# Keys of two chunks made together from pieces of the contraction, and the first norm of four tiles on ScalarE, in a post-norm transformer layer on eight cores

## The chip, the cores and the metric

The kernel runs on the 8 NeuronCores of one Trainium2 chip, one program on all of them, each core with its own data. The metric is the device time of the slowest core, in microseconds (us). Cores 0 to 3 are on one die, 4 to 7 on the other; the program has no exchange between cores.

## The reference

The layer takes x of shape (2, 4096, 2048) in fp32. `attn` and `ffn` stand for the two inner functions.

```python
def attn(x):                       # grouped keys and values, 4 groups of 128
    Q = x @ WQ.T + bQ              # 2048 wide, 16 heads of 128
    K = tile(x @ WK.T + bK)        # 512 wide, repeated 4 times
    V = tile(x @ WV.T + bV)        # 512 wide, repeated 4 times
    scores = einsum('btd,bsd->bts', Q, K)      # over all heads at once
    p = softmax(where(causal, -inf, scores)) / sqrt(128)
    return (p @ V) @ proj
def ffn(x):                        # 5632 wide
    h = silu((x @ gate_w.T) * gate_s) * ((x @ up_w.T) * up_s)
    return (h @ down_w.T) * down_s
x = layernorm(x + attn(x))
x = layernorm(x + ffn(x))
```

Since the keys are the same for all four repeats and the scores sum over all heads, the kernel folds WQ over its four repeats (three additions) and does the same with proj, so that queries, keys and values are all 512 wide.

## The kernel before

Four cores share one sequence of 4096 rows. Each core makes keys and values of the whole sequence for itself, in 8 chunks of 512 rows, and owns 8 tiles of 128 query rows, one from each chunk. Chunks 0 to 5 get real keys; chunks 6 and 7 are scored through the query times WK instead.

**Phases.** First keys (`k_outer`, `k_group`) and values (`v_outer`, `v_group`) of chunks 0 to 5, then the queries (`q_batch` for tiles 0 to 3, `q_tile` for the others), then attention of tiles 3, 2, 1, 0 and then 7, 6, 5, 4, each with scores, exponentials, transposes, values, projection, residual and norm; then gate and up of the feed-forward (L756), and last down (L939) with the second norm. The order on every engine is the order in which the program is written; a wait is on a semaphore of the writer.

**The start.** x and the weights lie in HBM in fp32 and are cast to bf16 by the transfers of the GpSimd queue (`load_piece`, L210). `wk` and chunk 0 (`xch[0]`) come in five pieces each, in turn, cut along the contraction at 0, 4, 8, 12, 14 and 16 of its 16 steps (`cuts0`). Chunk 1 is issued once the third piece of `wk` is there, `wv` once the last piece of chunk 0 is there, chunk 2 once the second piece of `wv` is there. `k_outer` makes the keys of a chunk with the pieces in the outer loop and the four column blocks `dq` in the inner one, so each block adds into its own PSUM bank; chunk 0 uses banks 0 to 3 and chunk 1 banks 4 to 7.

**The folds.** The fp32 pieces of WQ and proj (1 MB each, 32 of them) come on the SyncE queue into staging tiles `stg`, and VectorE folds each (L263 and L266) between its other work. `stage` issues the next load into a tile when its fold is done. `folds(n)` puts n of them at that place of VectorE's order.

**The norm.** `norm_a(i)` makes the reciprocal deviation on ScalarE (L701, L702), normalizes `y1` (fp32, 128 x 2048) on VectorE in place (L704) and stores it to `x1fd` (L707). `norm_b(i)` makes the bf16 copy `x1b` on ScalarE (L711), which `turn_x1` transposes on TensorE (L722). `load_xq` (L492) then fetches the residual of a later tile into the same `y1` buffer: tile order[m] goes into `y1` 0 or 1 in turn, and its load waits for the store of tile order[m-2]. SyncE issues stores and residual loads in program order.

Of the kernel before, what the change touches and what calls it, by code (L numbers as in the profile page):

```python
# [14 lines left out]
CT = 16  # L15
# [74 lines left out]
def build_program():  # L90
# [80 lines left out]
    def small(name, shape, dt=F32, size=4):  # L171
        nonlocal o
        t = sb(name, shape, dt, o)
        o += -(-math.prod(shape) * size // 32) * 32 / KB
        return t
# [16 lines left out]
    lnv = small("lnv", [2])  # L192
    rstd = small("rstd", [2])
    st2 = sb("st2", [NT, 5, 6], F32, 204)
    mv2 = sb("mv2", [NT, 2], F32, 205)
# [25 lines left out]
    for p, (lo, hi) in enumerate(zip(cuts0, cuts0[1:])):  # L221
        load_piece(wk, wkd, lo, hi, "wk%d" % p, t_wk)
        load_piece(xch[0], xT[0], lo, hi, "xa%d" % p, t_x[0])
    load_x(1, [t_wk[8]])
    for p in range(4):
        load_piece(wv, wvd, 4 * p, 4 * p + 4, "wv%d" % p, t_wv, [t_x[0][15]])
    load_x(2, [t_wv[7]])
# [43 lines left out]
    def folds(n):  # L271
        for _ in range(n):
            fold()
# [47 lines left out]

    def k_outer(j, cuts, b0):

        for lo, hi in zip(cuts, cuts[1:]):
            for dq in range(4):
                for ct in range(lo, hi):
                    tm = mm_k(j, dq, ct, b0 + dq, [t_wk[ct], t_x[j][ct]], ct == CT - 1)
                if hi == CT:
                    evac_k(j, dq, b0 + dq, tm)

# [46 lines left out]

    k_outer(0, cuts0, 0)
    k_outer(1, [0, 4, 8, 12, 16], 4)
    v_outer(0, 0)  # L380
# [5 lines left out]
    for j in range(1, HI):  # L386
# [24 lines left out]
        if j == 5:  # L411
            load_x(6, [t_kv[4], t_own[4], t_wq[12]])
            load_wkn(0, tk)
            load_x(7, [t_kv[5], t_own[5]])
            q_batch()
            q_tile(5, 5)
            folds(3)

# [280 lines left out]
    def norm_a(i):  # L699
        b, h = buf1[place[i]], place[i] % 2  # L700
        t1 = P.se(lambda e: e.activation(out=lnv[:, h:h + 1], in_=ve_[:, h:h + 1], func=AF.Ln), [t_stat[i]])  # L701
        t1 = P.se(lambda e: e.activation(out=rstd[:, h:h + 1], in_=lnv[:, h:h + 1], func=AF.Exp,  # L702
                                         scale=-0.5), [t1])
        t_n[i] = P.ve(lambda e: e.tensor_scalar(  # L704
            out=y1[b][:], in0=y1[b][:], scalar1=mv[:, h, 0:1], scalar2=rstd[:, h:h + 1],
# [3 lines left out]
    def norm_b(i):  # L709
        m, b = place[i], buf1[place[i]]  # L710
        t_x1b[i] = P.se(lambda e: e.activation(out=x1b[:], in_=y1[b][:], func=AF.Copy),  # L711
                        [t_n[i], t_xb_free, t_z[NT - 1]])
        if m + 2 < 6:
            load_xq(m + 2)
# [64 lines left out]
    v_group(6, 0, 0)  # L779
    folds(1)  # L780
    scores(3)
# [316 lines left out]
```

How the kernel before makes its waits and increments, by code:

```python
                def body(e, items=items):  # L74
                    seen = {}
                    for fn, waits, name, k in items:
                        for s, v in waits:
                            if seen.get(s, 0) < v:
                                e.wait_ge(self.sems[s], v)
                                seen[s] = v
                        if fn is not None:
                            ins = fn(e)
                            if name is not None:
                                ins.then_inc(self.sems[name], k)
```

## Time and profile before

| | us |
|---|---|
| three runs, median (lowest, highest) | 1292.86 (1292.38, 1535.46) |
| the profiled execution | 1292.36 |
| its span on core 7, the slowest | 1290.8 |
| spans of the eight cores | 1286.8 to 1290.8 |
| TensorE busy on core 7 | 1256.3 (97%) |
| VectorE busy | 328.7 (25%) |
| ScalarE busy | 172.9 (13%) |
| TensorE waiting for transfers at the start | 20.0 |

The span runs from the first to the last instruction of the core; the profiled execution's time is 1.6 us more than it. The highest of the three runs stands far above the two others, which agree within 0.04%. TensorE is busy for 97% of the span, so the profile is read for the places where it is not, and for what ends its waits there.

### The profile page before, as it was taken

Reading aid. Unit: us, or ns where it says so; the run is one execution under the profiler, and the core shown is the slowest. Engines: PE = TensorE matmul, PEld = TensorE weight load, DVE = VectorE, ACT = ScalarE, POOL = GpSimd, SP = SyncE. Lnnn points to the kernel's source line nnn. Section 1 sums busy time; section 2 is a strip of 40 time slices with the busy share of each in tenths; the row PEclk is TensorE's granted clock in tenths of the full one; section 3 lists DMA queues with packets and bytes.
Section 4 is the critical chain, followed back from the end, with each engine's and each line's share of the span. In section 5 each row is a group of like instructions: output and inputs, shape, how many; then the busy total and the mean of one; then the engine's idle time right before and its main releaser. Section 6 shows DMA issues by size and latency. Waiting matters only on the chain.

```text
span 1290.8 us, 15305 instructions; the slowest of 8 cores (1286.8 to 1290.8 us)
## 1 busy us (share of the span) xinstructions
PE 1256.3 (97%) x6316; PEld 589.7 (46%) x6316; DVE 328.7 (25%) x537; ACT 172.9 (13%) x269; POOL 73.9 (6%) x140
## 2 busy tenths in 40 slices
PE   4999999999999999999999999999999999999997
PEld 1444445654544444444444444444444444444444
DVE  0044435656873111011011011011010040130435
ACT  0100002333553101101101101100100000000001
POOL 2110000000000000001000000000000000000000
PEclk9999999999999999999999999999999999999999
DMA  9999999866881745545955445445405446464544
GB/s 145 166 254 267 235 195 268 247 152 117 222 221 73 131 67 88 87 86 91 169 103 88 72 69 90 71 69 88 71 1 115 79 70 145 79 143 80 120 124 189
DMA packets 33748, 166.10 MB, mean 129 GB/s; under 512 B 3984, under 2 KB 4112, under 8 KB 20240
## 3 DMA queue, kind: packets, MB, share of 16 engines
q0 software_dynamic: 19584, 96.48, 45.4%
q1 hardware_dynamic: 13808, 67.30, 15.4%
q10 hardware_dynamic: 288, 1.34, 0.3%
q8 instruction: 51, 0.84, 0.2%
q14 instruction: 17, 0.14, 0.0%
HBM read 244.80 MB, written 16.78 MB: 203 GB/s over the span
## 4 chain that ended last, share of the span: by engine, by line
PE 95%; DMA 3%; DVE 1%; issue 1%; ACT 0%; POOL 0%; DVEq 0%; ACTq 0%; POOLq 0%
PE pb L756 47%; PE pb L939 24%; PE pb L302 7%; PE pb L297 5%; PE pb L622 2%; PE pb L676 2%; PE pb L504 2%; DMA wk<-wkd 1%; DMA xch<-xT 1%; PE pb L366 1%; PE pb L351 1%; PE pb L510 1%; PE pb L563 1%; PE pb L454 1%; PE pb L722 0%
## 5 line engine op out<-in xcount | busy, mean ns | idle before, releaser
L756 PE MATMUL pb<-x1T,gu 128*128 128x512 bf16 x2816 | 609.1, 379 | 0.0
L756 PEld LDWEIGHTS pb<-x1T,gu 128*128 128x128 bf16 x2816 | 275.4, 98 | 331.0
L939 PE MATMUL pb<-dT,hT 128*128 128x512 bf16 (+2 forms) x1436 | 304.3, 375 | 0.4 <-DVE hT L774 0.4
L939 PEld LDWEIGHTS pb<-dT,hT 128*128 128x128 bf16 x1436 | 140.0, 98 | 164.8 <-issue 0.9
L774 DVE SCALAR_TENSOR_TENSOR hT<-pb,usc,sil 128x512 bf16<-128x512 f32 x88 | 66.1, 751 | 515.8 <-PE pb L756 515.8
L768 ACT ACTIVATE sil<-pb,gsc 128x512 f32<-128x512 f32 x88 | 60.5, 687 | 513.0 <-PE pb L756 512.9
L297 PE MATMUL pb<-xch,wk 128*128 128x512 bf16 x384 | 87.7, 389 | 20.0 <-DMA xch<-xT 20.0
L302 PE MATMUL pb<-wv,xch 128*128 128x512 bf16 x448 | 98.2, 379 | 0.0
L967 DVE SCALAR_TENSOR_TENSOR y<-pb,dsb 128x512 f32<-128x512 f32 x32 | 22.1, 691 | 216.0 <-PE pb L939 215.7
L297 PEld LDWEIGHTS pb<-xch,wk 128*128 128x128 bf16 x384 | 38.1, 100 | 68.5 <-issue 26.3
L302 PEld LDWEIGHTS pb<-wv,xch 128*128 128x128 bf16 x448 | 43.7, 98 | 52.4
L749 POOL DMA_DIRECT2D gu<-gud x46 | 26.0, 566 | 629.3 <-PE pb L756 587.5
L293 DVE TENSOR_TENSOR vv<-pb,bvb 128x512 bf16<-128x512 f32 x28 | 19.3, 690 | 120.2 <-PE pb L302 120.1
L263 DVE TENSOR_TENSOR stg<-stg 128x1024 f32<-128x1024 f32 x32 | 39.1, 1222 | 37.5 <-DMA stg<-wqd 25.9
L905 POOL DMA_DIRECT2D dT<-dnd x44 | 23.2, 534 | 286.3 <-PE pb L939 285.9
L985 ACT ACT_TABLE_LOAD x1 | 1.3, 1283 | 268.0 <-DVE lv L982 268.0
L504 PE MATMUL pb<-kT,qT 128*128 128x512 bf16 x132 | 32.2, 378 | 3.0 <-DVE lsc L517 1.7
L622 PE MATMUL pb<-vv,pt 128*128 128x512 bf16 x140 | 34.0, 379 | 1.0 <-DVE pt L569 1.0
L287 ACT ACTIVATE kT<-pb,bkc 128x512 bf16<-128x512 f32 x24 | 16.2, 687 | 124.0 <-PE pb L297 124.0
L676 PE MATMUL pb<-pjs,zT 128*128 128x512 bf16 x128 | 30.2, 379 | 0.0
L210 POOL DMA_DIRECT2D xch<-xT x33 | 17.7, 554 | 150.6 <-PE pb L297 54.6
L680 DVE SCALAR_TENSOR_TENSOR y<-pb,rec,y 128x512 f32<-128x512 f32 x32 | 23.1, 746 | 4.0 <-PE pb L676 1.3
(98 smaller groups left out, 453.2 us busy)
## 6 DMA issues: line engine op xcount, KB each, us to landing
gu<-gud POOLq DMA_DIRECT2D x46, 1024.0 KB, 10.3
dT<-dnd POOLq DMA_DIRECT2D x44, 512.0 KB, 6.3
stg<-wqd SPq DMA_DIRECT2D x16, 1024.0 KB, 24.6
stg<-prd SPq DMA_DIRECT2D x16, 1024.0 KB, 10.7
xch<-xT POOLq DMA_DIRECT2D x31, 512.0 KB, 17.6
y<-xq SPq DMA_DIRECT2D x8, 1024.0 KB, 8.3
x1fd<-y SPq DMA_DIRECT2D x8, 1024.0 KB, 7.2
x1r<-x1fd SPq DMA_DIRECT2D x4, 2048.0 KB, 14.2
```

Of the source, the lines that this page charges most:

```text
L263: t1 = P.ve(lambda e: e.tensor_add(stg[b][:, 0:2, :], stg[b][:, 0:2, :], stg[b][:, 2:4, :]), [tl])
L297: return P.pe(lambda e: e.matmul(bank[bk][:], wk[:, ct, dq * 128:(dq + 1) * 128], xch[XB[j]][:, ct, :], start=(ct == 0), stop=(ct == CT - ...
L302: return P.pe(lambda e: e.matmul(bank[bk][:], xch[XB[j]][:, ct, sv * 128:(sv + 1) * 128], wv[:, ct, :], start=(ct == 0), stop=(ct == CT - ...
L504: tm = P.pe(lambda e, c=c, dq=dq, bk=bk: e.matmul(bank[bk][:], qT[:, dq, i * 128:(i + 1) * 128], kT[c][:, dq, :], start=(dq == 0), stop=(d ...
L622: tm = P.pe(lambda e, c=c, r=r, j=j, first=first, last=last: e.matmul(bank[Z_BANK][:], pt[r][:, j, :], vv[c][:, j, :], start=first, stop=l ...
L676: tm = P.pe(lambda e, d=d: e.matmul(bank[pb][:], zT[i % 4][:, d, :], pjs[:, d, c * 512:(c + 1) * 512], start=(d == 0), stop=(d == 3)), [bf ...
L749: gu_at[it] = (s, P.dma("gpsimd", lambda e: e.dma_start(out=gu[s][:], in_=gud[it]), "gu%d" % s, list(waits) + [t_gu_free[s]]))
L756: tm = P.pe(lambda e, ct=ct: e.matmul(bank[bk][:], gu[s][:, w, ct, :], x1T[tch][:, ct, :], start=(ct == 0), stop=(ct == CT - 1)), [tg, bf[ ...
L768: ta = bf[gb] = P.se(lambda e: e.activation(out=sil[s][:], in_=bank[gb][:], func=AF.Silu, scale=gsc[:, it:it + 1]), [tm, t_sil[s], t_c["gs ...
L774: t_h[it][tch] = bf[ub] = t_sil[s] = P.ve(lambda e: e.scalar_tensor_tensor(out=hT[tch][:, it, :], in0=bank[ub][:], scalar=usc[:, it:it + 1 ...
L905: t_dT[s] = P.dma("gpsimd", lambda e: e.dma_start(out=dT[s % 8][:], in_=dnd[s // 11, s % 11]), "dT%d" % (s % 8), waits)
L939: return P.pe(lambda e: e.matmul(bank[tt if bk is None else bk][:, 0:hi - lo], hT[tt // 4][:, it, (tt % 4) * 128:(tt % 4 + 1) * 128], dT[s ...
```

## The change

1. `cuts0` also cuts chunk 1: its pieces are issued right behind those of `wk` and chunk 0, without a wait. `k_outer` works on both chunks for each piece of the contraction: 16 matmuls of chunk 0 (banks 0 to 3), 16 of chunk 1 (banks 4 to 7), and so on.
2. `wv` is issued when the fourth piece of chunk 0 (steps 12 and 13) is there, no longer the fifth.
3. One fold moves on VectorE from behind the first value group of chunk 6 (ahead of `scores(3)`) into the batch of queries: `folds(3)` becomes `folds(4)`.
4. For tiles 3 to 0 `norm_a` ends with a 128 x 1 instruction on VectorE (`nb`, minus mean times reciprocal deviation). `norm_b` makes `x1b` from the raw `y1` on ScalarE with scale and bias, then `y1` itself in place in a second pass, and only then issues the store. Tiles 7 to 4 are as before.

```diff
     for p, (lo, hi) in enumerate(zip(cuts0, cuts0[1:])):
         load_piece(wk, wkd, lo, hi, "wk%d" % p, t_wk)
         load_piece(xch[0], xT[0], lo, hi, "xa%d" % p, t_x[0])
-    load_x(1, [t_wk[8]])
+        load_piece(xch[1], xT[1], lo, hi, "xb%d" % p, t_x[1])
     for p in range(4):
-        load_piece(wv, wvd, 4 * p, 4 * p + 4, "wv%d" % p, t_wv, [t_x[0][15]])
+        load_piece(wv, wvd, 4 * p, 4 * p + 4, "wv%d" % p, t_wv, [t_x[0][13]])
...
-    def k_outer(j, cuts, b0):
+    def k_outer(cuts):
         for lo, hi in zip(cuts, cuts[1:]):
-            for dq in range(4):
-                for ct in range(lo, hi):
-                    tm = mm_k(j, dq, ct, b0 + dq, [t_wk[ct], t_x[j][ct]], ct == CT - 1)
-                if hi == CT:
-                    evac_k(j, dq, b0 + dq, tm)
+            for j in range(2):
+                for dq in range(4):
+                    for ct in range(lo, hi):
+                        tm = mm_k(j, dq, ct, 4 * j + dq, [t_wk[ct], t_x[j][ct]], ct == CT - 1)
+                    if hi == CT:
+                        evac_k(j, dq, 4 * j + dq, tm)
...
-    k_outer(0, cuts0, 0)
-    k_outer(1, [0, 4, 8, 12, 16], 4)
+    k_outer(cuts0)
...
             q_tile(5, 5)
-            folds(3)
+            folds(4)
...
+        if i < 4:
+            t_n[i] = P.ve(lambda e: e.tensor_scalar(
+                out=nb[:, h:h + 1], in0=mv[:, h, 0:1], scalar1=rstd[:, h:h + 1], scalar2=-1.0,
+                op0=OP.mult, op1=OP.mult), [t1])
+            return
...
     def norm_b(i):
-        m, b = place[i], buf1[place[i]]
-        t_x1b[i] = P.se(lambda e: e.activation(out=x1b[:], in_=y1[b][:], func=AF.Copy),
-                        [t_n[i], t_xb_free, t_z[NT - 1]])
+        m, b, h = place[i], buf1[place[i]], place[i] % 2
+        if i < 4:
+            t_x1b[i] = P.se(lambda e: e.activation(
+                out=x1b[:], in_=y1[b][:], func=AF.Identity, scale=rstd[:, h:h + 1], bias=nb[:, h:h + 1]),
+                [t_n[i], t_xb_free, t_z[NT - 1]])
+            t_n[i] = P.se(lambda e: e.activation(
+                out=y1[b][:], in_=y1[b][:], func=AF.Identity, scale=rstd[:, h:h + 1], bias=nb[:, h:h + 1]),
+                [t_x1b[i]])
+            t_st1[i] = P.dma("sync", lambda e: e.dma_start(out=x1f_r[i], in_=y1[b][:]), "x1f%d" % b,
+                             [t_n[i]])
+        else:
+            t_x1b[i] = P.se(lambda e: e.activation(out=x1b[:], in_=y1[b][:], func=AF.Copy),
+                            [t_n[i], t_xb_free, t_z[NT - 1]])
...
     v_group(6, 0, 0)
-    folds(1)
     scores(3)
```

The start on TensorE, before (`xch_66`, `xch_67` and `xch_68` are the buffers of chunks 0, 1 and 2; L297 makes keys, L302 values):

```order
L297 MATMUL pb<-xch_66,wk 128x512 x64
L297 MATMUL pb<-xch_67,wk 128x512 x64
L302 MATMUL pb<-wv,xch_66 128x512 x64
L302 MATMUL pb<-wv,xch_67 128x512 x64
L297 MATMUL pb<-xch_68,wk 128x512 x64
```

The same place of the changed kernel, whose line numbers are one higher here:

```order
L298 MATMUL pb<-xch_66,wk 128x512 x16
L298 MATMUL pb<-xch_67,wk 128x512 x16
L298 MATMUL pb<-xch_66,wk 128x512 x16
L298 MATMUL pb<-xch_67,wk 128x512 x16
L298 MATMUL pb<-xch_66,wk 128x512 x16
L298 MATMUL pb<-xch_67,wk 128x512 x16
L298 MATMUL pb<-xch_66,wk 128x512 x8
L298 MATMUL pb<-xch_67,wk 128x512 x8
L298 MATMUL pb<-xch_66,wk 128x512 x8
L298 MATMUL pb<-xch_67,wk 128x512 x8
L303 MATMUL pb<-wv,xch_66 128x512 x64
L303 MATMUL pb<-wv,xch_67 128x512 x64
```

The 128 matmuls of the keys are the same; they now follow the pieces of both chunks.

VectorE between the batch of queries and the first scores, before (`stg` are the staging tiles, `vv_55` the values of chunk 6, `lsc` the scores):

```order
L263 TENSOR_TENSOR stg_75<-stg_75 128x1024
L266 TENSOR_TENSOR pjs<-stg_75 128x512
L435 CAST bkh<-bkc 128x4
L436 TENSOR_TENSOR bkh<-bkc,bkh 128x4
L293 TENSOR_TENSOR vv_55<-pb,bvb 128x512
L263 TENSOR_TENSOR stg_69<-stg_69 128x1024
L266 TENSOR_TENSOR pjs<-stg_69 128x512
L517 TENSOR_SCALAR lsc,mx<-pb 128x512 x4
```

The same place of the changed kernel:

```order
L264 TENSOR_TENSOR stg_75<-stg_75 128x1024
L267 TENSOR_TENSOR pjs<-stg_75 128x512
L264 TENSOR_TENSOR stg_69<-stg_69 128x1024
L267 TENSOR_TENSOR pjs<-stg_69 128x512
L436 CAST bkh<-bkc 128x4
L437 TENSOR_TENSOR bkh<-bkc,bkh 128x4
L294 TENSOR_TENSOR vv_55<-pb,bvb 128x512
L518 TENSOR_SCALAR lsc,mx<-pb 128x512 x4
```

The fold of `stg_69` stands ahead of the evacuation of the first values of chunk 6, no longer between it and the first scores.

ScalarE at the norm of tile 0, changed kernel (`y_87` is `y1` 1; before there was one instruction, `L711 ACTIVATE x1b<-y_87`, in the place of the two 128x2048 ones):

```order
L702 ACTIVATE lnv<-vpe 128x1
L703 ACTIVATE rstd<-lnv 128x1
L719 ACTIVATE x1b<-y_87,nb,rstd 128x2048
L722 ACTIVATE y_87<-y_87,nb,rstd 128x2048
L746 ACTIVATE x1T_98<-pb 128x8x128
L785 ACTIVATE sil_114<-pb,gsc 128x512
```

The second pass stands between `x1b` and the copy of its transpose.

## Rows read from the trace of the kernel before

**Rows 1.** Waits of TensorE, whole run: line, what for, us in total, times, longest

```profile
PE pb L297 <- DMA xch<-xT: 20.0, 5, 12.7
```

**Rows 2.** Timeline of TensorE, 12 to 80 us: start, us, engine, line, [idle before <-releaser]

```profile
12.69 5.29 PE L297 MATMUL pb<-xch,wk 128*128 128x512 bf16 x16 [12.69 <-DMA xch<-xT]
...
26.18 7.03 PE L297 MATMUL pb<-xch,wk 128*128 128x512 bf16 x24 [3.47 <-DMA xch<-xT]
...
34.72 1.89 PE L297 MATMUL pb<-xch,wk 128*128 128x512 bf16 x8 [1.51 <-DMA xch<-xT]
...
37.85 13.97 PE L297 MATMUL pb<-xch,wk 128*128 128x512 bf16 x64 [1.24 <-DMA xch<-xT]
...
51.66 27.79 PE L302 MATMUL pb<-wv,xch 128*128 128x512 bf16 x128
```

**Rows 3.** Windows: stretch, busy us of six engines, granted clock, DMA share, GB/s

```profile
26.20:29.80 3.60, 3.60 (x9) 1.28 (x10) 0.00 (x0) 0.00 (x0) 0.00 (x0) 0.53 1.08 170
```

**Rows 4.** DMA queues, 20 to 40 us: packets, MB, share of 16 engines

```profile
q0 software_dynamic: 1181, 3.25, 101.6%
```

**Rows 5.** Line L210, its issues at 22.5, then 35.1, then 54.3 us

```profile
L210 POOL DMA_DIRECT2D xch<-xT x4: 532/552/567, 22.5 to 24.1; - x4
DMA to landing us min/median/max: 15.2/19.0/22.8
...
L210 POOL DMA_DIRECT2D wv<-wvd x4: 535/552/567, 35.1 to 36.7; - x4
DMA to landing us min/median/max: 14.8/19.4/23.0
...
L210 POOL DMA_DIRECT2D xch<-xT x4: 532/552/567, 54.3 to 55.9; - x4
DMA to landing us min/median/max: 10.4/15.8/23.9
```

**Rows 6.** Line L257, the staged load issued at 196.1 us

```profile
L257 SPq DMA_DIRECT2D stg<-prd x1: 327/327/327, 196.1 to 196.1; - x1
DMA to landing us min/median/max: 12.4/12.4/12.4
```

**Rows 7.** Timeline, all engines, 202 to 230 us

```profile
210.90 0.69 DVE L293 TENSOR_TENSOR vv<-pb,bvb 128x512 bf16<-128x512 f32 x1 [6.51 <-PE pb L302]
...
211.51 1.22 DVE L263 TENSOR_TENSOR stg<-stg 128x1024 f32<-128x1024 f32 x1
...
214.28 1.89 PE L504 MATMUL pb<-kT,qT 128*128 128x512 bf16 x8 [1.54 <-DVE lsc L517]
...
225.89 1.23 DVE L263 TENSOR_TENSOR stg<-stg 128x1024 f32<-128x1024 f32 x1 [1.23 <-DMA stg<-prd]
...
227.83 0.68 DVE L632 CAST lzn<-pb 128x512 bf16<-128x512 f32 x1
...
229.66 1.02 PE L504 MATMUL pb<-kT,qT 128*128 128x512 bf16 x4 [0.18 <-DVE lsc L517]
```

**Rows 8.** Timeline, all engines, 317 to 354 us

```profile
317.77 0.33 SPq L707 DMA_DIRECT2D x1fd<-y  x1
...
324.88 1.15 ACT L541 ACTIVATE upp<-usc__82,nmx 128x1024 bf16<-128x1024 f32 x1 [5.18 <-DVE nmx L522]
...
332.22 0.33 SPq L492 DMA_DIRECT2D y<-xq  x1
...
342.64 2.07 DVE L680 SCALAR_TENSOR_TENSOR y<-pb,rec,y 128x512 f32<-128x512 f32 x3 [1.31 <-DMA y<-xq]
...
345.18 1.02 PE L622 MATMUL pb<-vv,pt 128*128 128x512 bf16 x4 [0.97 <-DVE pt L569]
...
349.73 1.35 DVE L704 TENSOR_SCALAR y<-y,mv,rstd 128x2048 f32<-128x2048 f32 x1
...
351.17 1.91 ACT L711 ACTIVATE x1b<-y 128x2048 bf16<-128x2048 f32 x1 [1.55 <-DVE y L704]
...
353.23 1.05 PE L722 MATMUL pb<-idb,x1b 128*128 128x128 bf16 x16 [0.50 <-ACT x1b L711]
```

More of the change, by code:

```diff
@@ L193, in build_program @@
     rstd = small("rstd", [2])
+    nb = small("nb", [2])
     st2 = sb("st2", [NT, 5, 6], F32, 204)
```

## The prediction

> **What bounds the kernel now.** I read the waits of TensorE first. The engine is busy for 97% of the span, and of its idle time 20.0 us are one entry, keys waiting for `xch` [rows 1]. All of that lies ahead of 37.85 us. From there to the end of the span the remaining waits of TensorE add up to only a few microseconds, so whatever this change brings has to come out of the start, or out of a wait of the size of 1 us behind it.
>
> The timeline of the start [rows 2] shows the pattern: TensorE starts at 12.69 us, works off what has come, and stops before each further pair of pieces (3.47 us before 26.18, 1.51 us before 34.72, 1.24 us before 37.85). From 37.85 on it never stops for chunk 1 (64 matmuls in 13.97 us) and then runs the values of both chunks back to back from 51.82 (their first record starts at 51.66, behind a keys matmul still in the pipe). The spacing is 0.216 us per matmul at full clock (13.81 us for 64).
>
> The other side is the transfer engines. Between 20 and 40 us the GpSimd queue alone takes 101.6% of their time [rows 4]; they are full. The landings [rows 5] give the rate: the four pieces of chunk 1 land from 22.5 + 15.2 = 37.7 to 24.1 + 22.8 = 46.9 us, 3.1 us each; those of `wv` from 35.1 + 14.8 = 49.9 to 36.7 + 23.0 = 59.7, 3.3 us each; those of chunk 2 come last at 55.9 + 23.9 = 79.8. The change moves no byte away. It lets TensorE use chunk 1 while the same stream comes in.
>
> **The change part by part.**
>
> *Start.* `wk`, chunk 0 and chunk 1 are 12 pieces of 1 MB fp32 in both kernels, and the stream is full, so the last of them lands at about 46.9 us in both. Before, 64 matmuls of chunk 1 start at 37.85 and end at 51.82. Now all but the last 8 can be done when the last half piece lands: in the 34.2 us from 12.69 to 46.9 there is room for the other 120 (25.9 us, and 1.8 us more for the low rate of the first 16, which took 5.29 us). So the keys end at 46.9 + 8 x 0.216 = 48.6, 3.2 us earlier. This is the ceiling. Then the values of chunk 0 wait for `wv`: its first piece lands at 49.9, the last at 59.7, and 64 matmuls from 49.9 end at 63.7; before they end at 51.82 + 13.81 = 65.6. At unchanged landings the path gains 1.9 us. But two more pieces are halved. With four halves and the small `bvb` in the stream, the two units before 34.72 took 34.72 - 26.18 = 8.5 us where two take 6.2 later, 2.3 us more. A quarter of a piece of that, 0.8 us, is `bvb` itself; of the other 1.5 us for four halves, 0.8 us is my estimate for two more. That leaves 1.1. I take **1.5 us**, the middle; the ends are 0 (`wv` lands 1.9 us later) and 3.2 (`wv` lands earlier).
>
> The wait of `wv` for the fourth piece costs nothing: it comes about 6 us of queued stream ahead of the end of chunk 1. The next cover is chunk 2: its last piece (79.8) is used by the 13th matmul of its keys, now at 79.45 - 1.5 + 12 x 0.216 = 80.5. 0.7 us are left, so of a gain above 2.2 us the rest would wait there. Later chunks don't bind.
>
> *The moved fold.* At 211.51 VectorE folds between the values and the scores of tile 3 (1.22 and 0.69 us), and TensorE waits 1.54 us for a score bank [rows 7]. The data of that fold landed at 196.1 + 12.4 = 208.5 [rows 6], and VectorE then stands idle for 6.51 us up to 210.90 [rows 7]. So in its new place it is hidden, and the wait goes: 1.54 us. What is late next: the fold at 225.89 starts as its data lands (it waited 1.23 us), `lzn` stands behind it at 227.83, and the scores of tile 2 behind that; TensorE got its bank at 229.66 after only 0.18 us. The SyncE queue has a backlog there, so issuing one load 3 us earlier doesn't bring that data forward. With TensorE 1.5 us early the first score bank is read when `lzn` is done, 228.5 + 0.7 = 229.2. Of 1.54 us **0.45** are left. The ends are 0 and 1.54.
>
> *The norm.* For tile 0, L704 (1.35 us) [rows 8] leaves the chain to `x1b`; about 0.16 us for `nb` takes its place (as small VectorE instructions take here). `x1b` starts 1.2 us earlier and the wait of 0.50 us at 353.23 goes: **0.50 us**. The second pass costs ScalarE four times 1.91 us. Ahead of its next exponential it was idle for 5.18 us [rows 8], so that is hidden; without this cover each would cost 1.9 us. The Trainium skill, page "ScalarE: Activation LUTs", section "Rules for kernel authors", puts multiply and add on VectorE rather than ScalarE. The trace agrees on the durations, 1.35 against 1.91 us; on the path of four tiles that rule would make the sum 4 x 0.56 = 2.2 us worse. What speaks against that is the idle time of ScalarE; where it fails is the store, below.
>
> The store is the risky part. The store of tile 2 was issued at 317.77 and the residual of tile 0, which waits for it, at 332.22; it came in at 342.6, VectorE waited 1.31 us for it, and TensorE 0.97 us behind VectorE [rows 8]. The store now comes behind two passes of 1.91 us instead of one VectorE pass of 1.35 (plus 0.16): 2.6 us later. What it competes with are the first four loads of `gu`, issued behind the scores of tile 6. A later store leaves those more room early, they finish earlier, and the residual load then has the engines more to itself. I put the landing at 342.6 again, **0 us**, between -1.0 (the whole wait goes) and +2.6 (the delay is passed on).
>
> *Sum:* 1.5 + 0.45 + 0.5 = 2.45 us. The profiled execution took 1292.36 us, so 1289.9. That execution lies 0.5 us below the median of the runs shown (1292.86) and equals the fastest.
>
> **Rivals.**
>
> 1. *The store's delay is passed on.* Place: the residual of tile 0. If the store of tile 2 keeps its 14.4 us and the load its 10.4, the data comes at 345.2, TensorE loses 2.6 us there, and the sum is 2.45 - 2.6 = -0.15: 1292.5, and 1294.0 if the start brings nothing as well. It decides from a landing of 345.0 on. For: the wait was there already. Against: the load then competes with less. Beside it, the Trainium skill, page "DMA: Bandwidth & Descriptors", section "Queues, rings and completion order", says that an engine alternates between queues packet by packet; by that a store's share doesn't depend on when it starts, which gives this rival. Chance 0.22.
> 2. *The start brings nothing*, because more cut pieces slow the stream and `wv` lands 1.9 us later, or chunk 2 does. Then 0.45 + 0.5 remain: 1291.4. Chance 0.18.
> 3. *All of it arrives*: 3.2 + 1.54 + 0.5 + 1.0 = 6.2 us: 1286.1. It needs `wv`, chunk 2 and the staged data all earlier, against a full stream. Chance 0.08.
> 4. *The clock.* After the gap of 3.47 us the granted clock was 0.53 from 26.20 to 29.80 [rows 3], the lower of its levels (1.2 of 2.4 GHz), and 24 matmuls took 7.03 us in place of 5.2. A fall behind one of the new gaps costs up to 1.8 us; in the first 40 us it is waited away, behind the last key piece 1.3 us of it hide in the wait for `wv`. 1290.4. Chance 0.04, as the gaps get shorter.
>
> The forecast has 0.48.
>
> **Numbers.** Predicted 1289.9 us. The range reaches from 1287.2 (half of rival 3's surplus) to 1293.3 (rival 1 with part of a lost start). About 2% is what a measurement of this kernel can tell from no change, 26 us, and no case comes near it: faster 0.01, same 0.98, slower 0.01.
>
> **What would show it.** In the profile after: keys of both chunks end near 48.6 to 49.5 us, with gaps before each chunk 0 piece; values of chunk 0 start with a wait for `wv` and end near 64; no wait ahead of the keys of chunk 2. The wait of TensorE for `lsc` near 213 us is gone, and one for a fold's data shows near 228. `x1b` of tile 0 no longer holds its transposes. The wait of L680 for `xq` of tile 0 decides between forecast and rival 1. Wrong would be the forecast if the last piece of chunk 1 lands well after 46.9, or if a wait for staged data longer than 1 us stands ahead of the batch of queries.

## The result and the profile after: 0.18% slower, where 0.2% faster was forecast

The changed kernel took 1295.96 us in the median of 17 runs (lowest 1293.69), the kernel before 1293.08 us in the median of 17 runs beside it (lowest 1292.38). The ratio is 1.0018 with a 95% interval of [1.0011, 1.0025]: within 2%, but slower by more than the measurement's own uncertainty. The forecast was 1289.9 us, its range ended at 1293.3; the median lies 2.7 us outside. Both lists hold a few executions of 1345 us and more; the ratio leaves those out.

The profiled execution took 1296.2 us. The cores no longer agree as they did (the spans before were 1286.8 to 1290.8 us):

```profile
core 0: 1294.6 us, clock 0.995
core 1: 1286.0 us, clock 0.997
...
core 7: 1293.4 us, clock 0.997
```

Cores 1 and 5 (1285.7 us) are faster than any core before, core 0 is 3.8 us slower than the slowest. The mean of the eight spans rose by 1.7 us (1289.1 to 1290.8). So a little under half of the slowest core's loss in this execution is common to the cores, and the rest is that they lie farther apart.

**The waits of TensorE** on core 0, whole run (line, what for, us in total, times, longest), beside [rows 1]:

```profile
PE pb L298 <- DMA xch<-xT: 20.2, 5, 11.7
PE pb L505 <- DVE lsc L518: 2.2, 1, 2.2
PE pb L303 <- ACT kT L288: 2.0, 1, 2.0
...
```

The wait for the pieces is as long as before (20.2 against 20.0 us), the values now wait too, and one wait for a score bank has grown to 2.2 us.

**The timeline of TensorE at the start**, core 0 (start, us, engine, line, [idle before <-releaser]), beside [rows 2]:

```profile
11.66 8.64 PE L298 MATMUL pb<-xch,wk 128*128 128x512 bf16 x32 [11.66 <-DMA xch<-xT]
21.49 7.07 PE L298 MATMUL pb<-xch,wk 128*128 128x512 bf16 x31 [1.19 <-DMA xch<-xT]
34.20 12.76 PE L298 MATMUL pb<-xch,wk 128*128 128x512 bf16 x47 [5.65 <-DMA xch<-xT]
47.48 1.89 PE L298 MATMUL pb<-xch,wk 128*128 128x512 bf16 x8 [0.52 <-DMA xch<-xT]
50.58 1.89 PE L298 MATMUL pb<-xch,wk 128*128 128x512 bf16 x8 [1.21 <-DMA xch<-xT]
54.43 27.79 PE L303 MATMUL pb<-wv,xch 128*128 128x512 bf16 x125 [1.97 <-ACT kT L288]
```

The order works as written: 47 matmuls of both chunks run behind the gap, and only 16 are left for the last half pieces. But the last of those pieces is used at 50.58, so the keys end at 52.5, where I had 48.6, and the values start at 54.4. (One to three matmuls are missing from some records: x31, x47 and x125 stand for 32, 48 and 128.) Core 7, which was the slowest before, shows what they wait for:

```profile
53.82 27.90 PE L303 MATMUL pb<-wv,xch 128*128 128x512 bf16 x128 [1.90 <-DMA wv<-wvd]
```

On core 0 the row names ScalarE's evacuation of the keys, which ends about then; the last of the 16 engines delivers the first piece of `wv` at 54.2. In the mean of the eight cores the last key matmul starts 0.6 us earlier than before (its weight load at 49.98 against 50.60 us), but the first value then stands 2.2 us behind it, where it was 0.1: what the new order gave, the wait for `wv` took. Behind the gap of 5.65 us the clock is at its lower level again, beside [rows 3] (stretch, busy us of six engines, granted clock, DMA share, GB/s):

```profile
34.20:37.80 3.60, 3.60 (x9) 1.29 (x10) 0.00 (x0) 0.00 (x0) 0.00 (x0) 0.50 1.03 172
```

That is waited away here, as there is a wait for data behind it.

**The landings**, core 0: the half pieces issued at 7.4 to 9.0 us, beside [rows 5]:

```profile
L211 POOL DMA_DIRECT2D xch<-xT x3: 621/637/646, 7.4 to 9.0; - x3
L211 POOL DMA_DIRECT2D wk<-wkd x1: 629/629/629, 8.0 to 8.0; - x1
...
DMA to landing us min/median/max: 37.4/38.5/41.4
```

The last half piece lands at 9.0 + 41.4 = 50.4, not at 46.9.

**The batch of queries and the scores**, all engines, core 0, beside [rows 7]:

```profile
211.77 1.23 DVE L264 TENSOR_TENSOR stg<-stg 128x1024 f32<-128x1024 f32 x1 [5.26 <-DMA stg<-prd]
...
214.48 3.03 PE L505 MATMUL pb<-kT,qT 128*128 128x512 bf16 x12
...
229.66 1.23 DVE L264 TENSOR_TENSOR stg<-stg 128x1024 f32<-128x1024 f32 x1 [2.35 <-DMA stg<-prd]
...
231.60 0.68 DVE L633 CAST lzn<-pb 128x512 bf16<-128x512 f32 x1
...
233.04 1.19 PE L505 MATMUL pb<-kT,qT 128*128 128x512 bf16 x3 [2.21 <-DVE lsc L518]
```

The score bank at 214 is free in time now. The fold in front of `lzn` starts, as its data lands, 3.8 us later than before (229.66 against 225.89). Of these, 3.0 us are the later start of this core, but TensorE had won 1.4 us back at the score bank, so it waits here for 2.21 us. Behind that wait the granted clock falls to its lower level a second time, for 3.4 us from 233.3 (same columns as above):

```profile
233.00:236.60 3.60, 3.34 (x9) 1.31 (x11) 2.21 (x6) 0.76 (x1) 0.00 (x0) 0.55 0.70 257
```

Nothing waits for data behind this one, and it costs its full price, half of 3.4 us, 1.7 us. At this place only core 0 has it, the slowest of the eight; core 7 waited 1.87 us there and kept its clock.

**The norm and the residual of tile 0**, core 0, beside [rows 8]:

```profile
321.14 0.20 ACT L703 ACTIVATE rstd<-lnv 128x1 f32<-128x1 f32 x1
321.45 0.21 DVE L706 TENSOR_SCALAR nb<-mv,rstd 128x1 f32<-128x1 f32 x1 [1.70 <-ACT rstd L703]
321.76 2.10 ACT L719 ACTIVATE x1b<-y,nb,rstd 128x2048 bf16<-128x2048 f32 x1 [0.41 <-DVE nb L706]
...
323.95 2.10 ACT L722 ACTIVATE y<-y,nb,rstd 128x2048 f32<-128x2048 f32 x1
326.12 0.33 SPq L725 DMA_DIRECT2D x1fd<-y  x1
...
339.35 0.33 SPq L493 DMA_DIRECT2D y<-xq  x1
...
347.21 2.07 DVE L681 SCALAR_TENSOR_TENSOR y<-pb,rec,y 128x512 f32<-128x512 f32 x3 [0.79 <-DMA y<-xq]
```

Each pass takes 2.10 us, not 1.91. From the start of L703 to the store it is 4.98 us; the kernel before shows 1.73 us for the same on core 4:

```profile
313.31 0.20 ACT L702 ACTIVATE rstd<-lnv 128x1 f32<-128x1 f32 x1
...
315.04 0.33 SPq L707 DMA_DIRECT2D x1fd<-y  x1
```

So the store is 3.25 us later, where I had 2.6. Measured against TensorE's own work it is 3.24 us on all eight cores.

**Where the time went, as a sum.** TensorE issues the same 6316 weight loads in the same order from the values on, so the time between two of them can be subtracted. Mean of the eight cores of one profiled execution each, in us (worked out from the traces):

```
                          before   after   fold   norm   full pieces, wv ungated (e9)
up to the first value      50.72   52.19  51.39  51.99   48.77
values of chunks 0, 1      27.63   27.75  27.63  27.63   27.70
score bank near 213        11.22    9.89  10.63  11.22    9.89
fold's data near 228       16.60   17.73  16.93  16.84   17.92
residual, x1b of tile 0    50.91   51.22  50.94  52.08   50.76
all stretches, mean      1280.52 1282.41 1280.94 1283.09 1278.53
all stretches, slowest   1282.17 1286.40 1283.18 1285.03 1282.54
```

The first row moves by more than 1 us from one execution to the next in kernels whose start is the same: in the seven runs of this document that have the old start it is 50.7 to 52.4, and the profiled execution of the kernel before is the earliest of them. So it is read over several runs (in the part on the start below) and with the ratios. Of the slowest core's 4.2 us, 3.0 are start (54.40 against 51.44), 3.6 are the stretch near 228 (2.0 more of waiting and 1.7 of lower clock), and -1.4 and -0.9 come back at the score bank and at tile 0.

### The profile page after: what moved, and what is told of

Same layout as the page of the kernel before. It is cut to its first block, busy times and chain, and to the rows that moved or that the text cites. A ratio compares the mean times of both kernels' runs of the same rounds, so it can differ in the third digit from the quotient of the medians.

```text
span 1294.6 us, 15193 instructions; the slowest of 8 cores (1285.7 to 1294.6 us)
## 1 busy us (share of the span) xinstructions
PE 1252.3 (97%) x6198; PEld 590.0 (46%) x6316; DVE 324.3 (25%) x537; ACT 181.8 (14%) x273; POOL 74.8 (6%) x141
## 3 DMA queue, kind: packets, MB, share of 16 engines
q0 software_dynamic: 19728, 96.48, 43.3%
## 4 chain that ended last, share of the span: by engine, by line
PE 90%; DMA 6%; DVE 1%; issue 1%; POOL 1%; ACT 0%; DVEq 0%; ACTq 0%; SPq 0%; POOLq 0%
PE pb L773 47%; PE pb L955 23%; PE pb L303 6%; PE pb L298 4%; DMA stg<-prd 3%; DMA xch<-xT 3%; PE pb L623 2%; PE pb L677 2%; PE pb L505 2%; PE pb L511 1%; PE pb L564 1%; PE pb L368 1%; PE pb L739 1%; PE pb L455 1%; DVE stg L264 0%
## 5 line engine op out<-in xcount | busy, mean ns | idle before, releaser
L298 PE MATMUL pb<-xch,wk 128*128 128x512 bf16 x377 | 87.8, 391 | 20.6 <-DMA xch<-xT 20.2
L211 POOL DMA_DIRECT2D xch<-xT x34 | 18.3, 559 | 130.3 <-DVE xown L320 107.0
## 6 DMA issues: line engine op xcount, KB each, us to landing
xch<-xT POOLq DMA_DIRECT2D x30, 512.0 KB, 18.3
```

The costliest lines, as they stand in the source:

```text
L298: return P.pe(lambda e: e.matmul(bank[bk][:], wk[:, ct, dq * 128:(dq + 1) * 128], xch[XB[j]][:, ct, :], start=(ct == 0), stop=(ct == CT - ...
```

## The experiments

All were timed beside the kernel before, whose median was 1293.9 to 1294.2 us each time. Ratios are to the kernel before, with 95% intervals.

### One part at a time

e1 has points 1 and 2 of the change alone, e2 point 3 alone, e3 point 4 alone; their diffs are those pieces of the diff above.

> Only points 1 and 2 of the change (pieces of chunk 1 in the first stream, wv behind the fourth piece), the rest as before. Theory S (the start is where the time went: the values of chunk 0 begin with the landing of the first wv piece, 49.5 to 54.2 us over the cores in the changed kernel against 48.6 to 51.8 before): values of chunk 0 begin at 52 to 54.5 us on the slowest core, and the whole is 2 to 3 us slower than before, ratio 1.0015 to 1.0025. Theory N (the delayed store of tile 2, rival 1 of the prediction): the start is neutral or a gain, ratio 0.998 to 1.000.

> Only point 3 (the fold in the batch of queries). Theory S and the prediction's term: the wait of 1.5 us for a score bank near 213 us goes, up to 1.1 us of it comes back near 229 us, ratio 0.9990 to 1.0000. Theory F (the fold's data is late for a TensorE that comes early, and its new wait costs more than the old one): a wait of 2 us or more near 229 us, ratio above 1.0005.

> Only point 4 (norm of tiles 3 to 0 on ScalarE). Prediction's term: the wait of 0.5 us for x1b of tile 0 goes, the residual of tile 0 comes in at about the same time, ratio 0.9992 to 1.0002. Theory N: the residual of tile 0 lands up to 2.6 us later, VectorE waits 3 to 4 us for it and TensorE 2 to 3.5, ratio 1.0010 to 1.0020.

Measured: e1 1.0013 [1.0004, 1.0022], e2 0.9998 [0.9988, 1.0007], e3 1.0015 [1.0006, 1.0025]. Start and norm lose 1.7 and 1.9 us by themselves; the fold is neutral. The single parts add up to 1.0026, the whole is 1.0018; with intervals of 0.0007 to 0.001 to each side that is no contradiction. In the profiled executions the stretch of tile 0 takes 51.22 us in the whole and 52.08 with the norm alone, though TensorE comes to it at the same time in the mean (332.6 and 332.4 us); over the five kernels that have the new norm on all four tiles (e4 to e6 among them) it is 51.2 to 52.6.

### The start: which part of it

e4 is the whole change with `wv` not gated, e5 with the bias `bvb` loaded behind the keys, e6 with four full pieces in place of three full and two halves.

```diff
e4:
-        load_piece(wv, wvd, 4 * p, 4 * p + 4, "wv%d" % p, t_wv, [t_x[0][13]])
+        load_piece(wv, wvd, 4 * p, 4 * p + 4, "wv%d" % p, t_wv)
e5:
-    const("bvb", bvb[:], bvr.broadcast_to([128, DQ]), [t_x[0][4]])
+    const("bvb", bvb[:], bvr.broadcast_to([128, DQ]), [t_x[1][15]])
e6:
-    cuts0 = [0, 4, 8, 12, 14, 16]
+    cuts0 = [0, 4, 8, 12, 16]
```

> The changed kernel whole, but wv is issued right behind the first stream, without a wait. Theory S with the gate as its cause (wv is issued at 40 to 43 us, when the transfer engines that are ahead have already run dry): the first wv piece lands 1.5 to 3 us earlier than in the changed kernel, and the time falls by 1.5 to 3 us, ratio 0.9995 to 1.0008 against before. Theory H (halved pieces and pair contention slow the stream itself, the gate costs nothing): first wv piece lands within 0.5 us of the changed kernel's, ratio 1.0015 to 1.0025.

> The changed kernel whole, but the broadcast load of bvb (1 row to 128 partitions) is issued behind the last piece of chunk 1 in place of behind the second of chunk 0. Theory B (on one core of each pair that shares memory the stream falls from 170 to about 115 GB/s between 26 and 31 us because of this load): the dip at 26 to 31 us goes on all cores, eight pieces have landed at about 31 us on every core and no longer at 33 to 34 on four of them, the latest first values begin 1 to 2 us earlier, ratio 1.0003 to 1.0012 against before. Theory H (the halved pieces alone): dip unchanged or moved, ratio 1.0015 to 1.0022.

> The changed kernel whole, but wk, chunk 0 and chunk 1 come in four full pieces each; no piece is halved. Theory H (with six half pieces the 16 engines get out of step: the last piece of chunk 1 lands over 4 to 6.7 us, where a full piece lands over 1 to 2): spread of the twelfth piece below 3 us, first wv piece complete 1 to 3 us earlier, at 48.5 to 52, and ratio 1.0000 to 1.0010 although the last keys come as 32 matmuls behind the last piece. Theory B: spread falls, yet the slow core of each pair stays 2 us behind, ratio 1.0010 to 1.0018.

Measured: e4 1.0029 [1.0017, 1.0041], e5 1.0023 [1.0012, 1.0035], e6 1.0004 [0.9995, 1.0014]. Neither the gate nor the bias was the cause of the loss: with half pieces both edits leave it as it is or add to it. The bias does something else, though: with `bvb` late all eight cores move nearly the same number of bytes between 24 and 32 us (1.33 to 1.38 MB), as theory B of e5 said, and only its gain in time did not come (see the last section). Full pieces take most of the loss away, although the new norm is still in e6.

e7 has points 1 to 3 with the old norm, and e5's and e6's edits; it keeps the gate of `wv`. e10 is e7 with e4's edit, so without the gate. e9 is e10 with `bvb` in its old place, and e11 is e9 with `bvb` issued first of all:

```diff
e11:
-    const("bvb", bvb[:], bvr.broadcast_to([128, DQ]), [t_x[0][4]])
+    const("bvb", bvb[:], bvr.broadcast_to([128, DQ]))
```

> Points 1 to 3 of the change, the norm as before, with both cures: full pieces and bvb late. Theory S (start) says values of chunk 0 begin at 49 to 51 us on every core, and the whole is 1 to 3 us faster than before, ratio 0.998 to 0.999. If landings still reach 54 us on some core, neither of the two is the cause and the ratio stays at 1.001.

> Points 1 to 3 with full pieces, the norm as before, bvb where it was, and wv issued right behind the first stream. Theory G (with full pieces the wait of wv for the third-last piece leaves the engines without work: with the wait the stream carried 1.0 piece in 4 us behind the last piece of chunk 1, where 1.3 is usual): wv is complete at 56 to 59 us in place of 57 to 63, the keys of chunk 2 begin at or before 78 us on every core, ratio 0.9980 to 0.9990. If the broadcast of bvb is what starves wv, this kernel, which has it early, gains too, and the next one, which has it late, does not.

> As the kernel before it in this list, with bvb late (behind the last piece of chunk 1). Theory G: values of chunk 0 begin at 46.5 to 49.6 us and wv keeps up, keys of chunk 2 begin at 76 to 78 us, ratio 0.9975 to 0.9990. Theory P (the broadcast always takes one core of a pair down, and late it hits wv): values wait inside chunk 0 on half of the cores, ratio 0.9990 to 1.0000.

> As e9_full_free, with bvb issued first of all, without a wait. It costs the stream about 0.7 us at its head and no core should fall behind at 26 to 31 us. Theory P: the best of the three, first values at 48 to 50 us with a spread over the cores below 1.5 us, ratio 0.9975 to 0.9985. If the dip at 26 to 31 us has another cause, it stays and the ratio is that of e9_full_free.

Measured: e7 0.9999 [0.9990, 1.0008], e9 0.9982 [0.9972, 0.9991], e10 0.9981 [0.9971, 0.9991], e11 0.9988 [0.9978, 0.9998]. In e7 the first value starts at 47.9 us in the mean, but the values of the two chunks then take 30.6 instead of 27.6 us: the gate lets `wv` be issued only at 40.2 to 41.7 us (7.9 in e10), some 2 us before the last of the full key pieces is in (43.3 in the mean), and it comes late. This is core 0 of e7:

```profile
47.01 7.07 PE L302 MATMUL pb<-wv,xch 128*128 128x512 bf16 x31
57.42 23.73 PE L302 MATMUL pb<-wv,xch 128*128 128x512 bf16 x94 [3.35 <-DMA wv<-wvd]
```

e9 has no such gap, and 27.7 us. Here is its slowest core, 2:

```profile
12.67 8.46 PE L297 MATMUL pb<-xch,wk 128*128 128x512 bf16 x32 [12.67 <-DMA xch<-xT]
21.97 7.07 PE L297 MATMUL pb<-xch,wk 128*128 128x512 bf16 x31 [0.84 <-DMA xch<-xT]
34.46 16.40 PE L297 MATMUL pb<-xch,wk 128*128 128x512 bf16 x63 [5.42 <-DMA xch<-xT]
50.70 27.79 PE L302 MATMUL pb<-wv,xch 128*128 128x512 bf16 x125
```

From 34.46 on TensorE never stops. The gap's lower clock now stands on the path for a part of its price: 64 matmuls (one record is missing) took 16.4 instead of 13.8 us, while the first piece of `wv` was there at 49.5, 1.2 us before the values began. Core 2 is e9's slowest for a second reason, the one of core 0 above: it waits 2.28 us near 227 and its clock is then low for 3.4 us from 230.6. The same happens on the slowest core of e10.

e13 is e9 with the half pieces back, and nothing else:

```diff
-    cuts0 = [0, 4, 8, 12, 16]
+    cuts0 = [0, 4, 8, 12, 14, 16]
```

> e9 with one difference: wk, chunk 0 and chunk 1 are cut in five pieces each (six half pieces) instead of four full ones. Theory (the spread of the half pieces' landings costs the start): last key piece 2 to 4 us later than in e9, values of chunk 0 start at 51 to 53 us in place of 48.8, ratio 1.001 to 1.002 against 0.998 for e9. Rival (the gate of wv and the pair of cores were the cause, the cuts not): ratio 0.998 to 0.999 as e9.

Measured: 1.0006 [0.9997, 1.0016] against 0.9982 [0.9972, 0.9991], and the first value at 52.2 instead of 48.8 us. The price of six half pieces in place of three full ones is 0.24%, 3 us. The traces show two things. First the engines' rate, the GpSimd queue from 38 to 46 us (packets, MB, share of 16 engines), core 2 of e9:

```profile
q0 software_dynamic: 381, 1.37, 104.9%
```

and core 4 of e13:

```profile
DMA packets 528, 1.14 MB, mean 142 GB/s; under 512 B 59, under 2 KB 59, under 8 KB 528
...
q0 software_dynamic: 528, 1.14, 105.0%
```

The share is the same, the bytes are 17% fewer (13% in the mean of the cores), and a packet holds 2.2 KB on average instead of 3.6. On all eight cores it is 1.35 to 1.39 MB in e9 and 1.06 to 1.27 in e13 (1.33 to 1.38 before, 1.10 to 1.26 after), so a share of 100% does not tell how much comes. The median packet of 4096 bytes took 324 ns and that of 2048 bytes 173 ns, a little more than half; the means of all such packets in these 8 us are 399 ns (e9) and 247 ns (e13). Second the spread. A piece counts as landed when the last of 16 engines is done. The last key piece, and the first of `wv`, us (first and last engine, mean of eight cores, worked out from the trace's landings):

```
          last key piece: first  last   range of last    wv, first piece: last
before                     43.0   46.3   43.7 to 47.5                     49.4
after                      42.7   48.4   45.7 to 50.4                     52.0
e9                         43.3   45.0   42.6 to 47.1                     48.1
e13                        43.2   48.6   45.7 to 50.5                     52.0
```

The quickest engine is done at the same time in all four, within 0.6 us. The slowest is done 2.1 us later in the changed kernel than before: with the half pieces the engines drift apart, from 1.3 to 2.3 us apart (e9) to 3.8 to 8.7 us (e13). Since the execution of the kernel before is an early one, here are the same figures over all runs with the same cuts, whatever their norm, their bias and (with six half pieces) their gate (mean of the runs, us, worked out from the traces; the last column is the slowest core's):

```
                              last key piece        wv, first   first   keys of chunk 2
half pieces     runs     last engine  first to last     piece   value   mean   slowest
none, wv free      4            44.6            1.8      47.7    48.6   76.6      78.2
four, old order    7            47.0            3.8      50.1    51.5   79.2      80.5
six, new order     5            48.4            5.7      52.0    52.2   80.1      82.6
```

From four half pieces to six it is 1.4 us more at the last key piece, 1.9 us at the first piece of `wv`, and 2.1 us at the keys of chunk 2 on the slowest core, which is near the 1.7 us of e1's ratio. The drift was there in the kernel before too, 2.3 to 4.7 us at its last key piece, although its half pieces lie in the middle of the stream and four full ones follow: it is not made up behind them. It grows with the number of half pieces; whether their place matters as well was not tried. The Trainium skill, page "DMA: Bandwidth & Descriptors", section "Why a DMA increments its semaphore by 16 and not by 1", says that the 16 engines finish independently and the semaphore counts them; the landings here agree. The Trainium skill, same page, section "Specifications", asks for 512 B or more for the full rate; 469 of the 528 packets in this stretch of e13 hold 2 KB or more, and they still moved 17% less, so the trace does not bear that out for these casting loads.

### The norm: which part of it

e8 makes the new norm on ScalarE but normalizes `y1` first, stores it, and then makes `x1b`. e12 keeps the old norm and only lets the stores of tiles 3 to 0 wait for `x1b`, about 2 us more.

```diff
e8, norm_b, tiles 3 to 0:
+            t_n[i] = P.se(lambda e: e.activation(
+                out=y1[b][:], in_=y1[b][:], func=AF.Identity, scale=rstd[:, h:h + 1], bias=nb[:, h:h + 1]),
+                [t_n[i]])
+            t_st1[i] = P.dma("sync", lambda e: e.dma_start(out=x1f_r[i], in_=y1[b][:]), "x1f%d" % b,
+                             [t_n[i]])
+            t_x1b[i] = P.se(lambda e: e.activation(out=x1b[:], in_=y1[b][:], func=AF.Copy),
+                            [t_n[i], t_xb_free, t_z[NT - 1]])
e12, norm_b, tiles 3 to 0 (and no store in norm_a):
+            t_st1[i] = P.dma("sync", lambda e: e.dma_start(out=x1f_r[i], in_=y1[b][:]), "x1f%d" % b, [t_x1b[i]])
```

> Only point 4, but ScalarE normalizes y1 in place first, then the store is issued, then x1b is copied from y1. The store of tile 2 is then 0.7 us later than before, not 2.6, and x1b of tile 0 is ready 0.7 us later than before. Theory N (the loss of the norm part is the store's delay, passed on to the residual of tile 0): residual lands at most 1 us later than before, and ratio 1.0000 to 1.0008, against 1.0015 with the store last. If ScalarE's extra work itself costs, the ratio stays at 1.0015.

> The kernel before, with one edit: the stores of tiles 3 to 0 wait for the bf16 copy x1b (1.9 us later); no work moves between engines. Theory N (the store's place is what the norm part costs): TensorE takes about 1 us more from the scores of tile 4 to the first gate units, ratio 1.0006 to 1.0015. If ScalarE's second pass is what costs, this edit is free: ratio 0.9998 to 1.0003.

Measured: e8 1.0007 [0.9998, 1.0017], e12 1.0004 [0.9994, 1.0013]. Both ratios lie between 1 and e3's, and neither interval tells them from 1. In e8 the copy comes later: TensorE waits 1.5 us for `x1b` of tile 0 on every core, where it was 0.5. With the store 2.0 us later alone (e12) TensorE waits 0 to 1.4 us at tile 0, where it was 0 to 1.0, too little for the ratio to show. Neither settled it, so the norm was split by tiles: e14 takes the new norm for tiles 1 and 0 only (`if i < 2`), e15 for tiles 3 and 2 only (`if i in (2, 3)`), for whose stores the residuals of tiles 1 and 0 wait.

> The kernel before with the new norm on tiles 1 and 0 alone. Theory (the loss of the norm is the later stores of tiles 3 and 2, for which the residuals of tiles 1 and 0 wait): no loss here, the wait of TensorE for x1b of tile 0 (0.5 us) goes, ratio 0.9995 to 1.0000. Rival (the second pass on ScalarE itself holds later work, such as exponentials of tiles 0 and 7 or the copies of transposed x1): ratio 1.0008 to 1.0015, and a wait for ScalarE in the profile behind tiles 1 and 0.

> The kernel before with the new norm on tiles 3 and 2 alone. Theory (later stores): nearly the whole loss of the norm, ratio 1.0010 to 1.0020, DVE waits for xq of tile 0 of 2 to 3 us and TensorE for pt up to 3 us behind it, with the wait for x1b of tile 0 left as it was. Rival (second pass itself): about half the loss, 1.0005 to 1.0010, and e14 the other half.

Measured: e14 0.9994 [0.9984, 1.0003], e15 1.0020 [1.0011, 1.0030]. All of the loss is in tiles 3 and 2. Core 4 of e15, all engines:

```profile
321.48 0.33 SPq L724 DMA_DIRECT2D x1fd<-y  x1
...
336.29 0.33 SPq L493 DMA_DIRECT2D y<-xq  x1
336.71 0.39 SPq L713 DMA_DIRECT2D x1fd<-y  x1
...
345.30 2.07 DVE L681 SCALAR_TENSOR_TENSOR y<-pb,rec,y 128x512 f32<-128x512 f32 x3 [3.50 <-DMA y<-xq]
...
347.84 1.02 PE L623 MATMUL pb<-vv,pt 128*128 128x512 bf16 x4 [3.16 <-DVE pt L570]
```

The late store took 14.7 us, as in the kernel before (14.3 on core 7), and the residual was issued as soon as it was there. That came 8.9 us later, VectorE waited 3.50 us for it, and TensorE 3.16 us behind VectorE. Five of the eight cores of e15 show such a wait of VectorE, 2.2 to 3.5 us, and a sixth loses as much in that stretch; the stretch of the residual takes 53.9 us in the mean against 50.9. Of these 3.0 us some 1.1 are the clock again: on five cores (2 to 6) it stands at its lower level for 3.4 us behind the wait, from 347.6 to 349.1 on, 1.7 us each. On core 4:

```profile
347.80:351.40 3.60, 3.56 (x26) 2.74 (x27) 3.50 (x7) 1.39 (x2) 0.00 (x0) 0.64 0.74 200
```

How much of a store's delay is passed on can be read against TensorE's own work, too (worked out from the traces, means of all cores). In the ten kernels with the old store of tile 2 the residual of tile 0 lands 9.2 us behind one fixed weight load of TensorE ahead of it (8.5 to 9.6 by kernel); in the six where that store is 3.24 us later it lands 11.3 us behind (10.5 to 12.0). So 2.1 of 3.2 us are passed on: the store takes 14.3 us instead of 14.6, and the load behind it 7.7 instead of 8.5. In e12 0.5 of 2.0 us are passed on, in e8 0.8 of 1.05, each from one execution. Outside the start, the stretch near 228 and the one of tile 0 e15 loses nothing against the kernel before, so ScalarE's second passes themselves cost nothing there.

In e14 the stretch takes 50.5 us in the mean, and on its core 0 the transposes of `x1b` follow without a wait:

```profile
347.75 2.09 ACT L718 ACTIVATE x1b<-y,nb,rstd 128x2048 bf16<-128x2048 f32 x1 [0.41 <-DVE nb L706]
...
350.31 1.06 PE L738 MATMUL pb<-idb,x1b 128*128 128x128 bf16 x16
```

### A version that beats both

e16 is e9 with e14's half of the norm.

> e9 with the new norm on tiles 1 and 0. If e14 saves its 0.5 us, this gives 0.9978 (e9 gave 0.9982); if the second pass costs, 0.9990 or more. With TensorE earlier by 2 us at tile 0 the residual of tile 0 is waited for a little longer either way, and the 0.5 us of x1b may be swallowed there: then 0.9982.

Measured: 0.9981 [0.9972, 0.9990]. e9, e10 and e16 can't be told apart: 0.18 to 0.19% under the kernel before, with intervals clear of 1, some 2 us. They are faster than the changed kernel by about twice that.

## Why the prediction was wrong, step by step

Two of its steps failed, the start's and the store's; either alone measures a loss (e1, e3).

**Start: the first step that failed.** It was "the stream is full, so the last of them lands at about 46.9 us in both", with "0.8 us is my estimate for two more" half pieces as the only correction. The stream is as full as before by its share, but with six half pieces in the place of four it carried fewer bytes, and the engines lay farther apart at its end. The last key piece came 1.4 us later in the mean of the runs and the first piece of `wv` 1.9 us (52.0 against 50.1), 50.4 and 54.2 us on the slowest core. By the prediction's own sum 1.9 us would have left nothing of the gain, not made a loss. But that sum took the slack of `wv` from core 7 (49.9 against 51.82); in the mean of the seven runs with the old start it is 1.4 us, and the slowest core decides. The term was +1.5 with ends 0 and 3.2; alone it measured a loss of 0.13%, 1.7 us. The row that priced the four halves by the time between two units missed that a piece is there only with its last engine. Rival 2 named this cause, but stopped at "brings nothing". Nothing in the profile excluded a loss, so its end had to lie below nothing.

**"The wait of `wv` for the fourth piece costs nothing"** holds with half pieces only: ungating brought nothing in e4. With full pieces it costs 0.18% (e7 against e10).

**The order of the keys**, by which the last pieces leave only 8 or 16 matmuls, did what was written: the keys end earlier even in the changed kernel (by 0.6 us in the mean of the cores). That it is what gains in e9 is not shown apart: e9 has 2.0 us earlier values and 0.18%, but also full pieces and no gate, and no run has those with the old order. The ceiling of 3.2 us was not reached.

**The moved fold** went as forecast: the wait near 213 goes (11.22 to 10.63 in e2) and part of it comes back near 228 (16.60 to 16.93). Alone it is worth 0.26 us where I had 0.45, at a ratio of 0.9998. In the whole change more comes back, 1.1 us in the mean and 3.6 on the slowest core (1.7 of them the clock), in e9 as well. Why those staged loads do not come earlier with TensorE was not tried.

**The norm: the second step that failed.** The gain is where I put it: the wait for `x1b` of tile 0 is gone, and e14 stands at 0.9994 (my 0.5 us are 0.04%; its interval takes in 1). "I put the landing at 342.6 again, 0 us" was wrong, and rival 1 right in the main: the store kept its 13 to 15 us, and 2.1 of its 3.25 us of delay reached the residual (the load behind it got 0.8 us shorter, so the argument against rival 1 held for a part). The delay was 3.25 and not 2.6 us: 0.38 of the difference is that I took the passes at 1.91 us, the time of a plain copy, and the rest is the handing over between the engines and `nb`. With scale and bias from SBUF the passes take 2.10. The Trainium skill, page "ScalarE: Activation LUTs", section "What ACT_TABLE_LOAD costs", gives about 93 ns more for each such operand; 2.10 - 1.91 = 0.19 us agrees. Rival 1 had 1292.5 and a chance of 0.22; the loss of e3, 0.15% or 1.9 us, is near rival 1's 2.6 less the 0.5 us that the norm brings, partly by luck: less of the delay was passed on than rival 1 had, and the delay was longer.

**Second pass hidden by ScalarE's idle time:** right. e14 has it twice and loses nothing.

**The clock:** it fell behind the longer gap (0.50 from 34.2 to 37.8) and was waited away, as written. In e9 about 1.2 us of it is not (core 2). Rival 4 looked no further than the first gaps, which it expected to get shorter (the longest grew, from 3.47 to 5.65 us). The fall that cost 1.7 us came behind the longer wait near 228, on the core that sets the time.

**The sum.** Forecast 2.45 us gained; by parts the chip gave -1.7 for the start, +0.3 for the fold and -1.9 for the norm, -3.3 together, and -2.3 for the whole. Two slips are in the prediction's numbers: half of rival 3's surplus would end the range at 1288.0, not 1287.2, and its upper end of 1293.3 lies below a case that it had itself worked out, rivals 1 and 2 together at 1294.0. It also added to the one profiled execution (1292.36) and not to the median, which is 0.7 us higher over the 17 runs. None of this would have brought 1295.96 into the range.

## What to carry to other kernels

Price a transfer on the path by when its last engine is done, and not by the busy share of the queue. The engines drifted apart in every kernel that had half pieces, with those in the middle of the stream too, so cut a piece only where an earlier start is worth more. Before moving a store, look who waits for it; here two thirds of its delay arrived. Ask of each longer wait of TensorE also whether the clock falls behind it: in the changed kernel and in e9 that added 1.7 us on the slowest core. And when a change has a good idea and a cost in one edit, as here, take each out by itself: e9 keeps the order, drops the cuts and the gate, and wins what the change set out to win.

## What the runs showed of the hardware

- Half pieces (256 KB written, average packet near 2 KB instead of 3.6) moved 13% fewer bytes in the mean of the cores at the same share of the engines (e13 against e9, 38 to 46 us), and spread the landings of the 16 engines of one piece from 1.3 to 2.3 us to 3.8 to 8.7 us. That the drift is made by the cast and not by the size alone was not tried.
- In the four kernels compared for it (before, after, e9, e13) one core of each pair (0 and 1, 2 and 3, 4 and 5, 6 and 7) falls behind between 24 and 32 us. The GpSimd queue of core 0 of the changed kernel moved this much then:

```profile
q0 software_dynamic: 221, 0.83, 74.3%
```

and that of core 1:

```profile
q0 software_dynamic: 369, 1.34, 95.1%
```

All queues together it is 1.09 MB on core 0 and 1.60 on core 1. The difference of 0.5 MB is 3 us at 173 GB/s. Which core of a pair it is changes from kernel to kernel. It goes with the load of `bvb`, one row of HBM read for all 128 partitions, which is under way between 18.3 and 33.3 us in these four. Where `bvb` is issued at 42.6 us or later (e5, e7, e10), every core moves 1.33 to 1.39 MB in those 8 us; core 0 of e10:

```profile
q0 software_dynamic: 377, 1.38, 103.7%
```

In e5 the cores of a pair then differ from 52 to 60 us, while its `bvb` comes in (1.13 and 1.57 MB on cores 0 and 1, all queues), and in e11, where `bvb` is there by 8.2 us, they stay within 0.05 MB of each other in every 8 us from 16 to 56. Both cores of a pair together move 2.7 MB in 24 to 32 us with `bvb` in it (after, e9) and without (e10), so one core gets what the other lacks. Why the load divides them so is open. It did not decide the time: e9, e10 and e11, with `bvb` in its old place, late and first, have intervals that overlap.

- Behind a wait of TensorE of 2.2 to 3.2 us the granted clock was 0.50 for 3.4 us on core 0 of the changed kernel, core 2 of e9 and core 4 of e15, at a price of 1.7 us each. Behind one of 1.87 us (core 7 of the changed kernel) and one of 2.88 us (core 5 of e3) it did not fall, so the length of the wait alone does not tell.
